# A graph network's last layer: nine plain supertiles for eleven, a memset behind each plain gather, and two sums that alternate on TensorE

## The reference

```python
W_rel = jnp.matmul(w_comp, V).reshape(num_rels, in_dim, out_dim)   # 90 relations, 16 x 16 each
h_src = h[src]
e = jnp.concatenate([h_src @ Ws.T, he @ Ws.T, h[dst] @ Ws.T], axis=1) @ Wa.T
msg = jnp.einsum('ei,eio->eo', h_src, W_rel[rel_type]) * e
h_out = jax.ops.segment_sum(msg, dst, num_segments=n_nodes)
```

## Time and profile before

| | us |
|---|---|
| median of 3 runs | 3834.04 |
| lowest and highest | 3826.34, 3835.87 |
| the profiled execution's own time | 3831.75 |
| its span, first to last instruction | 3827.9 |
| start of the last layer in the trace | about 2565 |
| plain part (gathers of plain rows) | 2579 to 2707 |
| part with matmul and table supertiles | about 2700 to 3809 |
| closing additions and output | 3809 to 3828 |

### The profile page before, as it was taken

One profiled execution on the slowest core, in us unless ns is written; L12 is line 12 of the kernel. 1 busy time (PEld: TensorE's weight loads), 2 busy tenths in 40 slices (PEclk: granted clock), 3 DMA queues, 4 the chain that ended last, 5 costly groups with the idle time before them and its releaser, 6 DMA issues. The chain is left out here.

```text
span 3827.9 us, 79724 instructions
## 1 busy us (share of the span) xinstructions
PE 3464.6 (91%) x28788; PEld 2041.3 (53%) x28788; DVE 2825.9 (74%) x6513; ACT 1352.4 (35%) x2982; POOL 2060.6 (54%) x2942
## 2 busy tenths in 40 slices
PE   6878877999999978999999999667899999999997
PEld 4656654554455543555555554343566666666665
DVE  8999993232322137888888888456999999999997
ACT  6899990001100002333333333206222222222222
POOL 1000000784000006888888888416888888888884
PEclk8999997999899978999999999778999999999998
DMA  6444437856163474222222222389422222222222
GB/s 168 64 93 64 93 63 324 304 210 266 65 265 136 159 311 110 60 61 63 61 62 63 61 59 57 122 273 369 116 60 55 55 60 56 55 59 56 55 56 47
DMA packets 471492, 453.47 MB, mean 118 GB/s; under 512 B 355445, under 2 KB 402965, under 8 KB 459959
## 3 DMA queue, kind: packets, MB, share of 16 engines
q1 hardware_dynamic: 394582, 400.92, 33.7%
q0 software_dynamic: 50096, 37.33, 6.1%
q10 hardware_dynamic: 26417, 10.05, 1.0%
HBM read 353.92 MB, written 95.85 MB: 117 GB/s over the span
## 5 line engine op out<-in xcount | busy, mean ns | idle before, releaser
L1842 POOL DMA_INDIRECT rows<-typed_table,ring x576 | 659.2, 1144 | 172.9 <-POOL pause L1844 153.7
L1422 PE MATMUL L_ps<-ring,L_T 128*128 128x448 fp8e4 (+1 forms) x4606 | 671.1, 387 | 41.2 <-DMA ring<-adj 37.6
L2265 PE MATMUL l_ps_g<-ring,h_part 128*128 128x512 f16 x2568 | 627.7, 380 | 4.5 <-DVE l_tyh L2251 4.5
L1422 PEld LDWEIGHTS L_ps<-ring,L_T 128*128 128x128 f16 (+1 forms) x4606 | 328.0, 105 | 370.7 <-issue 61.0
L2271 ACT ACTIVATE l_sel<-l_ps_g 128x512 f16<-128x512 f32 x428 | 255.5, 597 | 704.6 <-PE l_ps_g L2266 704.6
L634 PE MATMUL cells<-keys,lows 128*128 128x147 f16 (+5 forms) x2744 | 373.0, 283 | 119.4 <-DVE keys L595 104.1
L1434 DVE SCALAR_TENSOR_TENSOR L_Y<-L_ps,L_scale,dinvB 128x448 f32<-128x448 f32 x84 | 57.4, 683 | 494.1 <-PE L_ps L1422 493.9
L2233 POOL DMA_INDIRECT ring<-typed_table,l_idxA x336 | 351.8, 1047 | 95.6 <-POOL pause L2235 94.2
L1904 DVE TENSOR_TENSOR dinvB<-G,tyh 128x1024 f16<-128x1024 f16 x260 | 307.2, 1222 | 128.4 <-ACT G L1891 128.4
L2233 POOL DMA_INDIRECT l_rows<-typed_table,l_idxA x336 | 347.1, 1033 | 99.1 <-POOL pause L2235 98.9
L634 PEld LDWEIGHTS cells<-keys,lows 128*128 128x128 f16 x2744 | 286.8, 141 | 202.9 <-DVE keys L595 170.5
(11 more groups left out here) (387 smaller groups left out, 5074.2 us busy)
## 6 DMA issues: line engine op xcount, KB each, us to landing
ring<-adj SPq DMA_DIRECT2D x67, 2744.0 KB, 11.1
adj<-ring SPq DMA_DIRECT2D x14, 2744.0 KB, 9.3
typed_table<-ring SPq DMA_DIRECT2D x49, 765.0 KB, 7.7
ring_fifth<-src_div_mod_rows SPq DMA_DIRECT2D x130, 256.0 KB
l_krow<-src_div_mod_rows SPq DMA_DIRECT2D x107, 256.0 KB
l_trow<-type_row SPq DMA_DIRECT2D x118, 180.0 KB
attr<-in_he POOLq DMA_DIRECT2D x25, 512.0 KB, 6.3
klast<-last_keys SPq DMA_DIRECT2D x86, 128.0 KB
```

The lines of the kernel that those rows point to most:

```text
L1422: ins = pe.matmul(bank[at:at + rows, 0:CH], d["T"][q][:, k, 0:rows], ring[r][:, k, :], start=n < side, stop=n >= NT - side, tile_position= ...
L1842: r_tok_[g] = r_in[b].by(pool.indirect_dma_start(rows[b][:, j, :], None, t1_dram, bass.IndirectOffsetOnAxis(ap=idxA[:, k * SUP + j:k * SUP ...
L2265: pe.matmul(ps_g[p][:, 0:HE], parts[p][:, j, :], hot[b][:, j, h * HE:(h + 1) * HE], start=j == 0, stop=False)
```

## The change

In words: `PLAIN` goes from 11 to 9 and `DIRECT` from 84 to 85, so there are 9 plain, 108 matmul and 85 table supertiles, and the loop has 117 steps' worth of supertiles instead of 118. The table tiles are made 12, then five a step, then the last two. Each of the 72 gathers of plain rows gets a memset of `pause` behind it, whose end POOL awaits before it goes on. `add_up` takes one or two supertiles; with two, their matmuls alternate, one of the one and one of the other. The table supertile behind i-2 now shares the `add_up` of i-2, so that it comes a quarter of the gather earlier, and both `put_sums` follow it. The neighbours' numbers differ by one, so that one uses the upper and the other the lower 64 partitions.

```diff
--- before.py
+++ after.py
@@ -68,7 +68,7 @@
 FU = F + 2
 XC = R90 * RC
 LEAD1, DIRECT1, ROWS_AHEAD = 3, 72, 12
-PLAIN, LEAD, DIRECT = 11, 2, 84
+PLAIN, LEAD, DIRECT = 9, 2, 85
 SPLIT_FROM = 4
 FIRST_TILES = 12
 BEYOND = 1 << 20
@@ -2218,6 +2218,7 @@
                 for j in range(SUP):
                     r_tok_[r] = r_in[RT - RG + b].by(pool.indirect_dma_start(
                         rows[b][:, j, 0:F], None, h_dram, bass.IndirectOffsetOnAxis(ap=srcA[:, r * SUP + j:r * SUP + j + 1], axis=0)), 16)
+                    link(pool, pool.memset(pause[:, :], 0.0))
 
             def fetch_table_rows(g):
                 b, k = g % RT, GK[g]
@@ -2347,14 +2348,20 @@
                 dve.wait_ge(*c_e.by(dve.tensor_tensor(eG[g % 2][:, :], rows[:, :, F], termA[:, k * SUP:(k + 1) * SUP], ALU.add)))
                 return c_rows.by(dve.tensor_tensor(rows[:, :, RC:MC], rows[:, :, 0:F], over(eG[g % 2][:, :], F), ALU.mult))
 
-            def add_up(k, dst, values, C, *toks):
-                h = k % 2
-                need(pe, *toks)
-                if k >= 2:
-                    pe.wait_ge(*sum_tok[k - 2])
+            def add_up(*supertiles):
+                for k, dst, values, C, toks in supertiles:
+                    need(pe, *toks)
+                    if k >= 2:
+                        pe.wait_ge(*sum_tok[k - 2])
                 for j in range(SUP):
-                    ins = pe.matmul(ps_a[h * WIN:(h + 1) * WIN, 0:C], dst[:, j, :], values[:, j, 0:C], start=j == 0, stop=j == SUP - 1, tile_position=(0, h * WIN))
-                a_tok[k] = c_a.by(ins)
+                    for k, dst, values, C, toks in supertiles:
+                        h = k % 2
+                        ins = pe.matmul(ps_a[h * WIN:(h + 1) * WIN, 0:C], dst[:, j, :], values[:, j, 0:C], start=j == 0, stop=j == SUP - 1, tile_position=(0, h * WIN))
+                        if j == SUP - 1:
+                            a_tok[k] = c_a.by(ins)
+
+            def by_rows(g):
+                return GK[g], dstG[g % 4], table_rows[g % RT], MC, (rows_tok[g], dstg_tok[g])
 
             def put_sums(k):
                 h = k % 2
@@ -2369,7 +2376,7 @@
                 act.wait_ge(*sum_tok[k])
                 o_out[h].by(act.dma_start(m3_dram[bass.ds(base, WIN), h, :], sums[h][at, :]), 16)
 
-            TILES = [0] + [FIRST_TILES + 4 * i for i in range(PLAIN - 1)] + [NT]
+            TILES = [0] + [FIRST_TILES + 5 * i for i in range(PLAIN - 1)] + [NT]
             need(sp, *[step(pool, pool.memset(trow[b][:, :], 0.0)) for b in range(2)])
             load_edges(0)
             h_tok = norm_of_spread(x_spread)
@@ -2425,16 +2432,17 @@
                     pool.wait_ge(*tab_tok[max(tiles), 2])
                     fetch_plain_rows(i + 1)
                 if i >= 2:
-                    k = EK[i - 2]
-                    add_up(k, dstP[(i - 2) % 3], msg[(i - 2) % 3], 2 * F, msg_tok[i - 2], dst_tok[i - 2])
-                    put_sums(k)
+                    add_up((EK[i - 2], dstP[(i - 2) % 3], msg[(i - 2) % 3], 2 * F, (msg_tok[i - 2], dst_tok[i - 2])),
+                           *[by_rows(g) for g in after[i - 2][:1]])
+                    put_sums(EK[i - 2])
+                    for g in after[i - 2][:1]:
+                        put_sums(GK[g])
                 if whole:
                     gather(i, 1, 1)
                 if i >= 2:
-                    for g in after[i - 2]:
-                        k = GK[g]
-                        add_up(k, dstG[g % 4], table_rows[g % RT], MC, rows_tok[g], dstg_tok[g])
-                        put_sums(k)
+                    for g in after[i - 2][1:]:
+                        add_up(by_rows(g))
+                        put_sums(GK[g])
             need(sp, *[(x.sem, x.n) for x in o_out])
             nc.all_engine_barrier()
             s.close()
```

## The result

The changed kernel takes **3811.14 us** (median of 4 runs, 3809.03 to 3815.04), the kernel before beside it 3834.95 us (3826.34 to 3838.72). The ratio is 0.9945, with an interval from 0.9931 to 0.9958. The forecast was 3817, with a range from 3796 to 3840. A second comparison gave 0.9941. On two other chips, where every kernel was slower, all kernels with the pair of sums lost to one with the sums apart; the experiments come to that. The changed kernel as it stands was not run on those two.

What follows compares the result with a forecast made beforehand. PE bounds the kernel; once it is faster, POOL ends the layer: 3789.3 + 3 + 0.5 + 1.8 + 18.4 = 3813.0 of span, 14.9 us less, so execution 3831.75 - 14.9 = 3817 us, range 3796 to 3840.

Steps and rivals of the forecast that it cites:

- The pair of sums: PE's table step: two alternating sums take 0.96 to 1.09 us together, so the step falls from 10.51 to about 9.35.
- ACT's order: ACT's copy of the gather's fourth quarter, now behind both sums: costs 0, at most 0.3 us a table step.
- the sign that the forecast named for a cost of this order: PE showing waits on ACT's `l_sel` before the fold would mean the ACT order costs what was put at nothing.
- Rival 4: PE before L2280, each table step: pair doesn't overlap and ACT's copy comes late; +30 us, execution 3861, chance 0.07.
- The plain part: Stretch before the table gathers, bound by DMA: last store at 2698, table gathers from 2699 against 2707.26, 8 us earlier.
- the memsets cost nothing: POOL's plain gathers go from 1.25 us to 1.44 to 1.603; hidden, with two supertiles less in a DMA-set part.
- DVE as a floor: Last layer, if DVE decides: start -2, one step more +10, waits -43, together -35 us; execution 3797, chance 0.17.
- POOL as the next bound: Last layer: 680 table gathers at 1.603 us, 1090 us from 2699, end at 3789 and decide; 14.9 us less, chance 0.48.
- the ending behind the last pair: From the last pair of sums to the end of the span: as before, 3827.9 - 3809.5 = 18.4 us.
- the window from 3785 to 3795: Where POOL's last gather should end, less than 5 us before its use, if POOL is the bound.
- The locked rhythm: POOL's gathers tied to DVE's steps, six in 9.84 us, 1.64 each; if such steps prevailed, 25 us more.
- rival 3: POOL slower: gathers at 1.62 to 1.64 us or start at 2703; +12 to +25, execution 3829 to 3842, chance 0.19.

Runs made afterwards that it cites:

- the first comparison: The changed kernel, as it stands, beside the kernel before on the same chip: 3811.14 us against 3834.95, ratio 0.9945.
- the second set: Changed kernel again (0.9941), one ACT copy moved back (0.994), 84 table supertiles (0.9915), 16-column memset (0.9905); the kernel before took 3837.72 us on that chip.
- the third set: Slowest chip, kernel before 4069.85 us: sums apart 0.9821, pair alone 1.011, no plain memset 1.0079, 84 table supertiles with 16-column memset and moved copy 1.0181.

## Why the prediction was right, step by step

- **The pair of sums.** Forecast 0.96 to 1.09 us for both, measured 1.08. PE leaves the path: its table step fits into DVE's 9.84.
- **ACT's order.** Forecast 0 to 0.3 us a table step, put at 0. The forecast had the copy of the last quarter end 0.1 us before the fold needs it. With the pair over at about 3207.97, it ends at 3210.42 + 0.60 = 3211.02, and PE's fold starts right behind it, at 3211.07; the loads of the fold waited for it, here and 73 times more (31.9 us). So the small margin was not there, and the sign that the forecast named for a cost of this order did show. Right was only that it doesn't reach the time, since DVE paces the step: the run with the copy moved back takes the same time within what can be told. Rival 4 named the right place, PE before the fold, with a price of 0.25 us and the pair's overlap as the trigger. On the slow chips the wait there is 2.4 us each time, and what sets it off is a semaphore of PE that comes late. Nothing in the trace of before, where it is on time, could have told that.
- **The plain part.** First one-hots forecast at 2698, measured 2696.34; first table gather 2699, measured 2696.99. The DMA share stays at 0.97 (1.01 in the earlier trace rows). That the memsets cost nothing agrees with these starts, but no run without them was made on a fast chip; on the slow ones they even brought about 10 us, which the forecast had not in it.
- **DVE as a floor.** Forecast -35 us if DVE decided; DVE does decide for the first half, with about 48.2 us for five steps.
- **POOL as the next bound.** Right, and it is the heart of the result: the lead is down to 2 us at the 44th table supertile. 680 gathers were taken at 1.603 us and took 1.594, 6 us less. The first came 2 us earlier. Together the last ends at 3781.2 and not at 3789.3: this is all of the difference of 8.0 us between the forecast span of 3813.0 and 3805.0. From there to the end 23.7 us were forecast and 23.8 measured, but that sum is right by luck in part: landing and start of weighing took 1.5 us (forecast 3), the ending behind the last pair 19.5 (forecast 18.4), and the two errors nearly cancel. The last gather ends 4 us before the window from 3785 to 3795 that the forecast gave as its sign.
- **The locked rhythm.** The forecast saw it, six gathers in a DVE step, and gave rival 3 the case that it costs 25 us. It isn't so strict: in the first half after, most steps of 9.84 us hold six gathers, but some hold seven and those of 8.84 five, and the first 384 gathers take 1.604 us each, as before. Where DVE has to wait, POOL's gathers go on in the gap at 1.44, and the rest take 1.586. The rule that I weighed there, from the Trainium skill's "SBUF — State Buffer", section "Who interferes with whom", has the two lock each other out for whole instructions. The trace agrees so far that the gathers beside the block take longer; they are not shut out for the whole block, since within that from 3206.46 to 3209.02 POOL starts a memset at 3207.06 and a gather at 3207.74. Why the gather is held for 2.17 us in place of 1.78 when the memset is short is not shown.

## What to carry to other kernels

When the busiest engine gets faster, look at what the next engine has in advance: the lead of a producer is a stock, and a forecast has to run it down supertile by supertile, not compare averages. Where the next in line is paced by a third one's bursts, making its own instruction shorter gives back only what falls outside the bursts (0.024 us of 0.09 here). And don't put a wait down to what is left over: look for the event that ended it. The distance between two uses of a buffer that is used once a step is the length of the step and says nothing of the cause. A rearrangement that wins half a percent on one chip can lose 3% on another, so it pays to measure on more than one.

## What the runs showed of the hardware that was not expected

- On two chips the semaphore behind PE's sums was raised a median of 1.2 to 2.9 us after the end of PE's rows while POOL issued gathers, and 0.013 us after it as soon as they had ended; in the first comparison and the second set it was 0.013 us throughout (medians). The stages ahead of the last layer took nearly the same time on all.
- A 64-row store of sums had the last of its landing events 1.7 to 3.1 us after its issue (medians of the first comparison and the second set), 5.5 at most.
- Interleaving two f32 sums on the two halves of the array costs no more than one of them: 1.08 us for 32 loads and matmuls, 1.05 to 1.12 for 16.
- A memset of 16 columns on POOL takes 0.12 us where one of 128 takes 0.22, and DVE's block of six one-hots beside it 2.46 us where it took 2.56. The wait of 0.27 us behind the memset stays.
- In one kernel of the third set PE's groups of matmuls started 0.7 to 1.4 us apart for a while with no wait shown: a slowness that no row names.
